# Decoder layer: the first normalisation's small operations in three groups, narrow transposes in 128 columns, and another order of work on all engines

## The reference, cut to what matters

```
x = x + softmax(-gamma * dist_sq) @ y1          # y1 = norm(x); dist_sq = |yi|^2 + |yj|^2 - 2 yi.yj
x = x + Wo(softmax(q k / sqrt(8) + slope_h * (i - j)) @ v) + bo   # q = norm(x) Wq + bq; 16 heads of 8; k, v of the context
mask = one_hot(top_2(softmax(y3 Wr + br)))      # y3 = norm(x), 8 experts
x = x + sum_e mask_e * (y3 @ W_e + b_e)
```

## Time and profile before

| | |
|---|---|
| median of 3 runs | 186.98 us (186.94 to 187.36) |
| profiled execution, its own time | 186.69 us |
| its span in the trace | 184.9 us |
| PE busy | 176.1 us (95%), 1494 matmul records |
| DVE busy | 149.9 us (81%) |
| ACT busy | 107.0 us (58%) |
| POOL busy | 67.8 us (37%) |
| PE clock granted | 9 tenths or more in all 40 slices |

### The profile page before, as it was taken

One profiled execution on the slowest core, in us unless ns is written; L12 is line 12 of the kernel. 1 busy time (PEld: TensorE's weight loads), 2 busy tenths in 40 slices (PEclk: granted clock), 3 DMA queues, 4 the chain that ended last, 5 costly groups with the idle time before them and its releaser, 6 DMA issues.

```text
span 184.9 us, 4330 instructions
## 1 busy us (share of the span) xinstructions
PE 176.1 (95%) x1494; PEld 118.4 (64%) x1500; DVE 149.9 (81%) x422; ACT 107.0 (58%) x219; POOL 67.8 (37%) x131
## 2 busy tenths in 40 slices
PE   6999999887999899999999999998999999999994
PEld 2456874666857677334643566655984577999893
DVE  4739989988999999998989798999815698398770
ACT  3049987989639846787876687763247850200100
POOL 6774813011638447305412000099201598010000
PEclk9999999999999999999999999999999999999999
DMA  5940069557275535433347000500006200010010
GB/s 93 344 141 0 9 141 238 125 160 210 64 197 141 104 90 157 121 111 84 104 115 154 9 7 11 232 9 0 2 15 194 90 4 0 2 60 0 32 56 29
DMA packets 20163, 16.89 MB, mean 91 GB/s; under 512 B 1645, under 2 KB 18165, under 8 KB 19865
## 3 DMA queue, kind: packets, MB, share of 16 engines
q1 hardware_dynamic: 20142, 16.62, 32.3%
HBM read 10.24 MB, written 6.37 MB: 90 GB/s over the span
## 4 chain that ended last, share of the span: by engine, by line
PE 72%; DVE 14%; DMA 5%; issue 3%; SPq 2%; ACT 1%; POOL 1%; ACTq 0%; DVEq 0%; POOLq 0%
PE bank L1485 15%; PE bank L1349 8%; PE bank L1387 7%; PE bank L1416 7%; PE bank L1230 6%; PE bank L1226 4%; DMA qs<-q_scratch 4%; DVE nm L1116 4%; PE bank L1295 3%; PE bank L1279 3%; DVE y L1007 3%; PE bank L1379 2%; SPq L560 2%; PE bank L1466 2%; PE bank L1412 2%
## 5 line engine op out<-in xcount | busy, mean ns | idle before, releaser
L1116 DVE TENSOR_REDUCE nm<-bank 128x3 f32<-128x462 f32 (+1 forms) x88 | 49.2, 613 | 2.9 <-PE bank L1349 2.8
L939 ACT ACTIVATE pt<-bank 128x512 f32<-128x512 f32 x80 | 43.7, 601 | 9.2 <-PE bank L1387 7.3
L1485 PE MATMUL bank<-ewT,ym 128*128 128x128 f32 x256 | 32.4, 278 | 0.0
L1485 PEld LDWEIGHTS bank<-ewT,ym 128*128 128x128 f32 x256 | 30.1, 192 | 0.6 <-POOL ym L824 0.4
L1349 PE MATMUL bank<-ks,qs 99*128 99x308 bf16 (+1 forms) x170 | 26.7, 263 | 1.5 <-DMA qs<-q_scratch 1.3
L1349 PEld LDWEIGHTS bank<-ks,qs 99*128 99x128 bf16 x170 | 13.7, 97 | 16.5 <-issue 5.9
L1387 PE MATMUL bank<-qs,ks 105*128 105x256 bf16 (+1 forms) x96 | 22.1, 310 | 0.2 <-DVE nm L1116 0.2
L1007 DVE TENSOR_SCALAR y<-xs,mv,rs 128x128 f32<-128x128 f32 x48 | 18.5, 438 | 0.2
L807 POOL TENSOR_SCALAR ve<-mv 128x2 f32<-128x2 f32 (+1 forms) x6 | 1.3, 214 | 47.2 <-DVE mv L1002 47.1
L1416 PE MATMUL bank<-pt,vm 128*32 128x256 f32 (+1 forms) x192 | 18.5, 462 | 0.0
L824 POOL TENSOR_TENSOR ym<-mask_all,y3T 128x512 f32<-128x512 bf16 x16 | 18.2, 1172 | 0.0
(11 more groups left out here) (141 smaller groups left out, 282.1 us busy)
## 6 DMA issues: line engine op xcount, KB each, us to landing
mask_all<-e_scratch SPq DMA_DIRECT2D x2, 1024.0 KB, 5.0
ks<-k_scratch SPq DMA_DIRECT2D x4, 480.0 KB, 4.6
q_scratch<-qpart SPq DMA_DIRECT2D x8, 192.0 KB, 2.1
qs<-q_scratch SPq DMA_DIRECT2D x8, 192.0 KB, 3.8
xs<-in_x_dram SPq DMA_DIRECT2D x4, 256.0 KB, 4.1
q_scratch<-qpart SPq DMA_DIRECT2D x8, 128.0 KB, 2.6
qs<-q_scratch SPq DMA_DIRECT2D x8, 128.0 KB, 3.3
k_scratch<-mask_all SPq DMA_DIRECT2D x4, 240.0 KB, 3.0
```

Source lines behind the costliest of these rows:

```text
L939: nc.scalar.activation(pt[:, n % RING, :], at("scores", b, i)[:, :], ACT.Exp).then_inc(exps, 1)
L1116: v.tensor_reduce(nm[b][:, n:n + heads], at("maxima", b, g)[:, 0:heads * J].rearrange("p (s j) -> p s j", s=heads), AX.X, ALU.max, negate= ...
L1485: last = mm(at("experts", b, p)[:, tile(t)], ym[:, e, tile(t)], ewT[:, e, :], start=False, stop=(e == E - 1), skip_group_check=True)
```

## The change

1. `FIRST` goes from (1, 3) to (1, 1, 2): `rstd1` and `squares` on POOL run in three groups, batch 0, batch 1, batches 2 and 3.
2. The transposes of the squares and of the row maxima read 128 columns, of which all but 3 and 48 are zero: `sqp` grows to 128 columns, `mcat` too, and there are two tiles `mcat` used in turn where there were four. DVE sets them to zero in its first step. `mcat` of batches 2 and 3 waits until the transpose of two batches before has read the tile.
3. `ORDER`, `TURNS` and `WARM` are new. On PE, steps of 32 columns now stand together more often.
4. Paths that nothing used are taken out (`STACKED`, `ADDED`), and `SPREAD` is written as `MASKS`; with `MASKS = "ppss"` the work for the mask is the same as before.

```
-SPREAD = (2, 3)
-FIRST = (1, 3)
+MASKS = "ppss"
+FIRST = (1, 1, 2)
...
 ORDER = {
     "tensor": """
-        start:0.0 y1T:0.0 sqT:0.0 dist:0.0 dist:0.1 dist:0.2 keys:0.0 dist:0.3 y1T:1.0 keys:0.1 key_values:0.0
+        start:0.0 y1T:0.0 keys:0.0 keys:0.1 key_values:0.0 sqT:0.0 dist:0.0 dist:0.1 dist:0.2 dist:0.3 sqT:1.0
...
 WARM = {
-    "y1T:0.0": 28, "sqT:0.0": 4, "probs:1.0": 1, "probs:2.0": 2, "maxima:1.0": 3,
+    "y1T:0.0": 26, "probs:0.0": 4, "sqT:1.0": 1, "y2T:0.0": 1, "maxima:1.0": 6,
 }
...
-        sqp = sb("sqp", [P, B, T, 3], BF16)
+        sqp = sb("sqp", [P, B, T, P], BF16)
...
-        mcat = each("mcat", [P, T, 3, H], BF16)
+        mcat = two("mcat", [P, T, P], BF16)
...
 def squares(g_, _):                                  # POOL
+                pool.wait_ge(sq_set, 1)
...
 def setup(b, _):                                     # DVE
                 v.memset(idle[:, :], 1.0).then_inc(idle_set, 1)
+                v.memset(sqp[:, :, :, :], 0.0).then_inc(sq_set, 1)
                 for i in range(2):
                     v.memset(sqT[i][:, :], 0.0).then_inc(sq_set, 1)
+                for i in range(2):
+                    v.memset(mcat[i][:, :, :], 0.0).then_inc(sq_set, 1)
...
 def mcat_(b, p):                                     # DVE
-                part = [mcat[b][:, t, i, :].rearrange("p t (s a) -> p t s a", s=2) for i in range(3)]
+                part = [mcat[b][:, t, i * H:(i + 1) * H].rearrange("p t (s a) -> p t s a", s=2) for i in range(3)]
+                if b >= 2:
+                    dve.wait_ge(mT_ps, through(PARTS3, b - 2, PARTS3[b - 2] - 1))
...
 def sqT_(b, _):                                      # PE
-                flip(range(T), col16(at("sqT", b))[0:3], lambda t: sqp[:, b, t, :], ident16).then_inc(sqT_ps, 1)
+                flip(range(T), col16(at("sqT", b)), lambda t: sqp[:, b, t, :], ident16).then_inc(sqT_ps, 1)
...
 def mT_(b, p):                                       # PE
                 pe.wait_ge(mcat_ready, through(PARTS3, b, p))
-                flip(tiles(PARTS3, b, p), col16(at("mT", b, p))[0:3 * H],
-                     lambda t: mcat[b][:, t, :, :].rearrange("p i h -> p (i h)"), ident16).then_inc(mT_ps, 1)
+                pe.wait_ge(sq_set, 5)
+                flip(tiles(PARTS3, b, p), col16(at("mT", b, p)), lambda t: mcat[b][:, t, :], ident16).then_inc(mT_ps, 1)
```

More of the change, by code:

```diff
@@ L74 @@
     """,
     "gpsimd": """
[L76 to L80, removed]
@@ L81 @@
-        select:1.5 select:1.6 select:1.7 rstd3:3.0 rstd3:3.1
+        setup:0.0 gamma:0.0 rstd1:0.0 bias:0.0 squares:0.0 rstd1:1.0 squares:1.0 zeros:0.0 y1g:1.0 rstd1:2.0
+        rstd2:0.0 squares:2.0 y1g:2.0 rstd2:0.1 weights:0.0 rstd2:1.0 rstd2:1.1 x1b:0.0 x1b:1.0 y1g:3.0
+        rstd2:2.0 split:1.0 split:1.1 split:2.0 rstd2:2.1 expert_bias:0.0 split:2.1 x1b:2.0 rstd2:3.0 rstd2:3.1
+        split:3.0 x1b:3.0 split:3.1 rstd3:0.0 rstd3:1.0 select:0.0 select:0.1 select:0.2 select:0.3 select:0.4
@@ L104 @@
+        aoT:3.1 mask:2.1 y3T:3.1 mask:3.0 mask:3.1
     """,
     "vector": """
[L106 to L114, removed]
@@ L125 @@
-        select:2.1 wo:3.1 select:2.2 select:2.3 select:2.4 y3:3.1 select:2.5 route:3.0 select:2.6 select:2.7
-        route:3.1 store:2.0 select:3.0 select:3.1 select:3.2 select:3.3 store:2.1 select:3.4 select:3.5
-        select:3.6 store:3.0 select:3.7 store:3.1
+        setup:0.0 stats1:0.0 k_zeros:0.0 y1:0.0 stats1:1.0 keys:0.0 dist:0.0 dist:0.1 dist:0.2 dist:0.3
+        rowmax:0.0 y1:1.0 stats1:2.0 keys:0.1 stats1:3.0 key_values:0.0 gather:0.0 dist:1.0 dist:1.1 dist:1.2
+        y1:2.0 dist:1.3 y2:0.0 key_values:0.1 gather:0.1 rowmax:1.0 key_values:0.2 key_values:0.3 split:0.0
@@ new lines @@
+        y2:0.1 dist:2.0 dist:2.1 dist:2.2 tail_values:0.0 dist:2.3 rowmax:2.0 split:0.1 gather:1.0 gather:1.1
+        y1:3.0 y2:1.0 y2:1.1 gather:2.0 maxima:0.0 maxima:0.1 maxima:0.2 maxima:0.3 maxima:0.4 maxima:0.5
+        maxima:0.6 dist:3.0 y2:2.0 maxima:0.7 dist:3.1 maxima:0.8 maxima:0.9 maxima:0.10 maxima:0.11
+        maxima:0.12 dist:3.2 dist:3.3 maxima:0.13 rowmax:3.0 maxima:0.14 maxima:0.15 maxima:0.16 maxima:0.17
+        maxima:0.18 maxima:0.19 maxima:0.20 maxima:0.21 gather:2.1 mcat:0.0 maxima:1.0 maxima:1.1 y2:2.1
@@ L501, in step3, with by_dve, all_masked @@
             return k // 2, k % 2
-        def stacked(b, a, who):
-            return STACKED.index(b) * COPIED.count(who) + COPIED[:a + 1].count(who)
+        def by_dve(b):
+            return E * sum(m != "p" for m in MASKS[:b])
+        def all_masked(b):
+            return (masked, E * (b + 1)) if MASKS[b] == "p" else (masked_last, by_dve(b) + E)
         def released(name, b, k):
```

409 lines of the change are left out of this document (178 added, 231 removed).

## The result

The changed kernel took 184.46 us (median of five executions) beside 186.98 us: ratio 0.985 [0.982, 0.988]. The gain is 2.5 us; 6.6 were predicted. 184.46 lies inside the range and near rival 3's 183.7, but for another reason than rival 3's.

The account below looks back on a forecast made before the run. PE was taken to bound the middle and the end; 2.0 + 4.6 = 6.6 us off the profiled 186.69 gives 180.1, and 0.3 more for the median 180.4 us. Range: 176.5 to 184.8 us.

Parts of the forecast that it names:

- rival 3: Between first and last maxima: DVE becomes the bound, PE's other 3.3 us become waits; 183.7 us, chance 0.14.
- Price of a change: On PE, where the number of columns changes: 0.11 us each, range 0.08 to 0.14, for the 60 counted ones.
- 18 changes behind the last maxima: PE's end: 18 x 0.11 = 2.0 us saved, counted in full as PE bounds there.
- 42 in the middle: Between first and last maxima: 42 x 0.11 = 4.6 us saved on PE, counted in full.
- rival 4: First stage gains 2.6 us (177.8 us), or the y3:1.0 collision vanishes (177.1), or a little of both (176.5); chance 0.15.
- the added waits on `mcat`: mcat of batches 2 and 3 waits for a transpose of two batches earlier, long done: nothing.
- Rounds of 64 rows: On PE, four new neighbours of 64 and 128 rows: bounds 0 to 0.6 us, taken as 0.
- rival 1: Rounds of 64 rows cost like a change of columns: 4 x 0.11 on top, 180.8 us, chance 0.15.
- Three groups: Some ten small operations more on POOL, which is 37% busy: nothing.
- First stage's order: Keys moved ahead of batch 0's row maxima and split on DVE: between +1.6 and -2.6 us, taken as 0.
- Transposes in 128 columns, zeroing: Wider weight loads on PE, 0.4 us at most, and DVE's zeroing, 0.2 us sticking out at most: both nothing.
- Rival 6: Longer narrow runs on PE starve DVE, eight waits of about 1.12 us: slower, 188.5 us, chance 0.07.

Follow-up runs that it names:

- the mended kernel: The changed kernel with one wait more on POOL, so that batch 0's select begins only when mcat:3.0 is ready: 180.77 us, ratio 0.966.

## Why the prediction was wrong

- **Price of a change** (0.11 us, read as 0.08 to 0.14): right on the spot, too high in the total, where it was counted in full. Three edits of 16 or 17 changes gave 0.06, 0.07 and 0.07, each from a difference of 1.0 to 1.2 us that is known to several tenths. The 60 counted changes are then 4.2 us and not 6.6: this term was 2.4 us too large.
- **18 changes behind the last maxima, 2.0 us in full; 42 in the middle, 4.6 us in full**: that they count was right in both places, since PE bounds in both once the collision is gone (+2.3 for 2.1 us of products in the middle, +1.8 for 1.7 in the end); that they count in full was not. At the end 0.28 of 1.66 us fell into a wait for DVE; for the middle that was not looked up.
- **Rival 3, DVE becomes the bound of the middle**: wrong as a mechanism, though its 183.7 us lies near. The sign named for it, idle PE waiting for DVE, did come, but as one wait of 2.05 us for the slowed `mcat:3.0`; without the collision 1.8 us more on DVE cost 0.4. That 184.46 lies inside the range by way of this rival is luck.
- **The collision**: this is the step that failed, a path and a wait that the sum did not have. I used the 4.42 us of `y3:1.0` only as room for DVE and in rival 4 as something that might vanish; the sum had no term for it. It holds two. The old victim got free, worth 1.6 us in the kernel before. And I never asked what stands in the 9 us of `select` in the new order: `mcat:3.0`, on which PE waits at once. That cost 3.05 us, 2.05 of it the hole; the rest fits the clock behind it. Net of the old victim it is 1.5 us, so that of the 4.1 us missing some 2.4 belong to the price of a change and 1.5 to the collision. The order lists told which steps were near; I argued only that the added waits on `mcat` were "long done".
- **Rounds of 64 rows**, taken at 0: four times 0.14, 0.6 us on the spot; rival 1.
- **Three groups**, taken at nothing: 0.7 us lost in the old order. In the new one the squares of the third group stand behind `y1g:1.0`; whether they cost anything there was not tried.
- **First stage's order**, taken at 0: its beginning on DVE gains 0.9 us, measured against the old beginning beneath the other engines' new lists.
- **Transposes in 128 columns, zeroing**: nothing for loads and zeroing, right; with them 16 changes go, 1.0 us.
- **Rival 6**: no long wait of DVE came; between the first and the last `maxima` of the changed kernel the longest was 0.44 us.

The account: between the two kernels freed of their collisions, 0.992 and 0.966, lie 4.8 us; 64 changes at 0.07 make 4.5; the gain of DVE's new beginning (0.9) and the cost of the rounds of 64 rows (0.6) nearly cancel. Add 1.6 for the old victim and the forecast of 6.6 is nearly met, 6.4, by 180.77 us measured. Take off 3.05 for the new victim and 3.3 is left, beside 3.1 by the ratio of the changed kernel's second measurement and 2.5 in its first. The parts were measured in different kernels and are known to several tenths of a us each, so that they add up this well is in part luck. That 180.4 nearly met the mended kernel is thus partly two errors that cancel: a dear change and an uncounted collision.

## What to carry to other kernels

When an order changes, list for each long POOL operation on SBUF what DVE does in that time, before and after, and ask who waits for it; a victim that gets free leaves its place to the next. If the place matters, hold the patient engine with a wait rather than trust in the order: here one wait on POOL was worth 3 us, and the order alone broke with 2 us more on PE. An engine that is 96% busy bounds nothing until a load on it shows in the time; add one to each engine, in a version where no single collision can carry it.

## What was not expected of the hardware

- Behind a hole of 2 us in PE's work the granted clock fell to 1.2 GHz for about 3.4 us in the execution that was profiled, and the mean clock was 0.98 or 0.99 in 10 of the changed kernel's 11 executions, 1.0 in one; behind 3 of 4 us idle it stayed there for about 10 us (190.6 us, hole and clock together, where the fastest execution of the same kernel took 182.4).
- DVE's small operations on SBUF (0.2 us) each lasted about as long as one of POOL's (1.1 us) beside it, but for the first of them, 0.3 to 0.9 us; reductions from PSUM did not.
- A change of rows, 128 to 64, at the same columns cost 0.14 us on the spot, like one of columns.
